# Values projected as rows of keys in one product with the keys, their step found by folds and two TensorE transposes

## The reference

```python
q = (x @ Wq + bq).reshape(1, B * N, H, hd)
kv = (cond @ Wkv + bkv).reshape(1, -1, 2, H, hd)
k, v = (kv[:, :, 0], kv[:, :, 1])
q = _fq_sym(q, axis=-1)      # rounded to 127 steps of the row's own maximum
k = _fq_sym(k, axis=-1)
v = _fq_sym(v, axis=2)       # one step for each channel, from the maximum over all 5776 keys
attn = jax.nn.softmax(jnp.einsum('bhqd,bhkd->bhqk', q, k), axis=-1)
attn = _fq_unsigned(attn, axis=-1)
out = jnp.einsum('bhqk,bhkd->bhqd', attn, v)
```

## Time and profile before

| | us |
|---|---|
| median of 3 runs | 1885.77 |
| the runs | 1884.38 to 1887.85 |
| the profiled execution, its own time | 1881.91 |
| its span | 1880.1 |
| VectorE busy | 1694.6 (90%) |
| TensorE busy | 1644.0 (87%) |
| GpSimd busy | 1450.3 (77%) |
| ScalarE busy | 1373.7 (73%) |
| 16 DMA engines, share of the span | 79.4% |

### The profile page before, as it was taken

The page is one execution under the profiler, slowest core; times in us unless marked ns, Lnnn a source line. Parts: engine busy times, 40 slices in busy tenths (PEclk is TensorE's granted clock), DMA queues, the critical chain, the costliest instruction groups (busy, mean ns, idle before and its releaser), DMA issues.

```text
span 1880.1 us, 40526 instructions
## 1 busy us (share of the span) xinstructions
PE 1644.0 (87%) x16216; PEld 1131.0 (60%) x16216; DVE 1694.6 (90%) x2665; ACT 1373.7 (73%) x1326; POOL 1450.3 (77%) x1190
## 2 busy tenths in 40 slices
PE   7997889888898888889888888888988888789998
PEld 6884666665566666655666666444455455468776
DVE  6869999999999999999999999999999999986665
ACT  2447889888888988887888888877778888732222
POOL 1442899988999988989989889899898799652232
PEclk9999999997699999977999999756589999889999
DMA  5668889997999799969897999798988998841231
GB/s 175 214 209 200 173 171 206 190 191 149 177 189 194 158 199 181 189 139 193 171 207 159 177 189 200 123 172 161 175 167 160 190 194 160 162 117 44 66 58 46
DMA packets 851527, 309.88 MB, mean 165 GB/s; under 512 B 784966, under 2 KB 813964, under 8 KB 851212
## 3 DMA queue, kind: packets, MB, share of 16 engines
q1 hardware_dynamic: 851340, 307.29, 79.4%
HBM read 74.26 MB, written 39.59 MB: 61 GB/s over the span
## 4 chain that ended last, share of the span: by engine, by line
DVE 44%; PE 22%; POOL 11%; DMA 8%; issue 7%; ACT 6%; SPq 1%; POOLq 0%; DVEq 0%; ACTq 0%
DVE S L1159 39%; POOL PT L1388 8%; DMA PP<-Pr 6%; PE PS L776 5%; ACT Pr L973 4%; PE PS L657 4%; PE PK L813 3%; PE PK L598 2%; PE PS L625 2%; PE PK L600 1%; PE PO L600 1%; PE PO L598 1%; POOL VV L1333 1%; PE PO L676 1%; DVE kam L1058 1%
## 5 line engine op out<-in xcount | busy, mean ns | idle before, releaser
L1159 DVE TENSOR_SCALAR_CACHE_REDUCE S<-PS,SQN 128x1536 f32<-128x1536 f32 (+1 forms) x768 | 1285.0, 1713 | 45.1 <-PE PS L657 37.5
L973 ACT ACTIVATE Pr<-S,MS 128x5888 uint8<-128x5888 f32 x200 | 1041.3, 5207 | 207.2 <-DVE MJ L1185 143.1
L1388 POOL CAST PT<-PP 128x1536 uint16<-128x1536 uint8 (+1 forms) x800 | 1100.7, 1420 | 112.0 <-DMA PP<-Pr 109.3
L657 PE MATMUL PS<-KT,QT 96*128 96x512 bf16 (+1 forms) x2496 | 711.7, 410 | 141.5 <-DVE S L1159 127.3
L676 PEld LDWEIGHTS PO<-VI,PT 128*128 128x128 f16 x9200 | 354.1, 99 | 226.0 <-issue 79.7
L657 PEld LDWEIGHTS PS<-KT,QT 96*128 96x128 bf16 (+1 forms) x2496 | 206.3, 104 | 354.4 <-issue 164.0
L676 PE MATMUL PO<-VI,PT 128*128 128x32 bf16 x9200 | 365.5, 180 | 11.4 <-ACT AO L923 8.0
L598 PE MATMUL PK<-WG,CT 128*128 128x128 f32 (+1 forms) x1288 | 217.9, 300 | 46.1 <-ACT VV L839 38.8
L600 PE MATMUL PK<-CT,WG 128*128 128x128 f32 (+1 forms) x1288 | 213.2, 294 | 0.0
L598 PEld LDWEIGHTS PK<-WG,CT 128*128 128x128 f32 (+1 forms) x1288 | 171.8, 197 | 52.4 <-issue 51.2
L600 PEld LDWEIGHTS PK<-CT,WG 128*128 128x128 f32 x1288 | 168.5, 194 | 1.7 <-issue 0.6
(11 more groups left out here) (149 smaller groups left out, 1501.6 us busy)
## 6 DMA issues: line engine op xcount, KB each, us to landing
CT<-ctxt SPq DMA_DIRECT2D x180, 256.0 KB, 3.2
k_rows<-KS SPq DMA_DIRECT2D x44, 512.0 KB, 4.1
q_rows<-QS SPq DMA_DIRECT2D x13, 512.0 KB, 4.2
W13F<-w13T SPq DMA_DIRECT2D x12, 352.0 KB, 3.7
PP<-Pr SPq DMA_TRANSPOSE x200, 5.9
XT<-x SPq DMA_DIRECT2D x12, 256.0 KB, 3.3
XR<-x SPq DMA_DIRECT2D x12, 256.0 KB, 3.4
base_rows<-XO SPq DMA_DIRECT2D x12, 256.0 KB, 3.4
```

The lines of the kernel that those rows point to most:

```text
L657: last = pe.matmul(PS[n % 2][p0:p0 + r, f:f + w], QT[h % 3][0:PARTS * HD, q0:q0 + r], KT[h % 3][0:PARTS * HD, c * CHUNK + f:c * CHUNK + f ...
L973: act.activation(Pr[i % 2].rearrange("p t q b -> p t b q"), S[i % 2].rearrange("p (t b q) -> p t b q", b=2, q=P), ACT.Exp, bias=MS[:, i % ...
L1159: v.tensor_scalar(S[i % 2][:, c * CHUNK:c * CHUNK + CW[c]], PS[n % 2][:, 0:CW[c]], neg_step, None, ALU.mult, ALU.min, accum_out=MN[:, i % ...
L1388: gp.tensor_copy(PT[i % 2][:, 2 * t0:2 * t1, :].rearrange("p (t b) q -> p t b q", b=2), PP[i % 2][:, t0:t1, :].bitcast(U8).rearrange("p t ...
```

## The change

- **One product for keys and values.** A unit is now four float32 products with the context as the stationary operand and 256 columns, 128 of key weights and 128 of value weights, and one bias product of 256 columns before the last of them. Values come out as rows of keys, as the product with the attention weights wants them. The last unit is padded to 128 rows. The bias tiles are twice as wide; VectorE makes the parts of group 0 first and those of the other groups (768 columns) after the second `layernorm`.
- **The step of a channel.** Channels now lie along the row. `batch` takes the maximum over the four units of a batch for each of 128 channels (512 elements in, 128 out, the inner step 512 bytes), into one of five slots of `VM`. After batches 3, 6, 9 and 11 VectorE folds four slots into one (`V_FOLD`, again 512 in, 128 out, behind the last chunk of the step). TensorE transposes the 128x128 of maxima (`max_turn`), `v_step` reduces it out of PSUM, ScalarE spreads the reciprocal over a row (`scale_spread`), TensorE transposes it back (`scale_turn`) and ScalarE copies the row of scales to `VS` (`scale_out`).
- **Rounding.** `v_quant` is now a multiplication of two tensors (values by the broadcast `VS`) and the addition and subtraction that rounds, written straight to `VI`. It begins 1.2 steps later. Group 0 is rounded by it too, on GpSimd, 12 batches at the end of the front.
- **Removed:** the 36 DMA transposes of `turn_v`, the three of group 0 with ScalarE's `value_ints`, four small loads of the values' bias, four memsets of `VB` on GpSimd.

```diff
-                for c in slices:
-                    for d in range(2 * (c % 2), 2 * (c % 2) + 2):
-                        if c < 2:
-                            pe.matmul(bank[0:n, 0:GC], CT[k % RING][:, d, 0:n], WG[:, d, 0, :], start=(d == 0), stop=False)
-                        else:
-                            last = pe.matmul(bank[:, GC:GC + n], WG[:, d, 1, :], CT[k % RING][:, d, 0:n],
-                                             start=(d == 0), stop=(d == NK - 1))
...
+                for d in slices:
+                    last = pe.matmul(bank, CT[k % RING][:, d, :], WG[:, d].rearrange("p a c -> p (a c)"),
+                                     start=(d == 0), stop=(d == NK - 1))
+                    if d == NK - 2:
+                        if u == 0 and g < 2:
+                            pe.wait_ge(M["s_b3"], g + 1)
+                        pe.matmul(bank[0:n], ones[:, 0:n], BK3[:, 2 * GC * g:2 * GC * (g + 1)], start=False, stop=False)
...
+            def max_turn(g):
+
+                pe.wait_ge(M["s_vm"], len(V_FOLD) * (g + 1))
+                pe.wait_ge(M["s_kve"], (g + 1) * NU)
+                pe.transpose(v_bank(g)[:, 0:GC], VM[:, 0, :], ident[:, :]).then_inc(M["s_vmt"], 1)
+
+            def scale_turn(g):
+
+                pe.wait_ge(M["s_vbc"], g + 1)
+                pe.transpose(v_bank(g)[:, GC:2 * GC], VM[:, 1, :], ident[:, :]).then_inc(M["s_vst"], 1)
...
-                        for r in range(VRING if g else 0):
-                            pe.wait_ge(s_vb[r], 16 * (NBT * g // VRING))
-                        pe.wait_ge(M["s_vi"], 16 * len(VT_LO))
+                        pe.wait_ge(M["s_vg"], NBT * (g + 1))
...
+                    if i in v_step_of and c == 2:
+                        max_turn(v_step_of[i])
+                    if i - 2 in v_step_of and c == 1:
+                        scale_turn(v_step_of[i - 2])
...
+            def scale_spread(g):
+
+                act.wait_ge(M["s_vr"], g + 1)
+                act.wait_ge(M["s_vmt"], g + 1)
+                act.activation(VM[:, 1, :], ones[:, :], ACT.Copy, scale=VS3[:, g % 2, 2:3]).then_inc(M["s_vbc"], 1)
+
+            def scale_out(g):
+
+                act.wait_ge(M["s_vst"], g + 1)
+                if g:
+                    act.wait_ge(M["s_vg"], NBT * g)
+                act.activation(VS, v_bank(g)[:, GC:2 * GC], ACT.Copy).then_inc(M["s_vs"], 1)
...
-                vals = VV[b][:, 0:w] if g else VF[:, us[0] * P:us[0] * P + w]
-                chain.mark(v.tensor_reduce(VMX[:, g % 2, b:b + 1], vals, X, ALU.max, apply_absolute_value=True))
+                vals = VV[b] if g else VF[:, us[0]:us[-1] + 1, :]
+                slot = b if b < NB else (b - NB) % (NB - 1) + 1
+                if b == 0 and g:
+                    v.wait_ge(M["s_vst"], g)
+                chain.mark(v.tensor_reduce(VM[:, slot, :], vals.rearrange("p n c -> p c n"), X, ALU.max,
+                                           apply_absolute_value=True))
...
+                if b in V_FOLD:
+                    lo = V_FOLD.index(b) % 2
+                    v.tensor_reduce(VM[:, (1 - lo) * NB, :], VM[:, lo:lo + NB, :].rearrange("p n c -> p c n"), X,
+                                    ALU.max).then_inc(M["s_vm"], 1)
+                    v.wait_ge(M["s_vm"], len(V_FOLD) * g + V_FOLD.index(b) + 1)
...
             layernorm(0)
             layernorm(1)
+            bias_parts(1, NG)
...
-                        if b == NBT - 1:
-                            v_step(0)
+                    if t == Q_HEAD + 1:
+                        v_step(0)
...
-                    gp.wait_ge(M["s_vr"], g + 1)
-                link(gp.tensor_scalar(q, q, VS3[:, g % 2, 2:3], MAGIC, ALU.mult, ALU.add))
-                if k >= NBT + VRING:
-                    gp.wait_ge(s_vb[k % VRING], 16 * ((k - NBT) // VRING))
-                gp.tensor_scalar(VB[k % VRING][:, 0:w], q, 1.0, -MAGIC, ALU.mult, ALU.add).then_inc(M["s_vg"], 1)
+                    gp.wait_ge(M["s_vs"], g + 1)
+                    if g >= 2:
+                        gp.wait_ge(M["s_pv"], PHASE * (g - 1))
+                link(gp.tensor_tensor(q, q, VS.unsqueeze(1).to_broadcast([P, n, GC]), ALU.mult))
+                gp.tensor_scalar(VI[g % 2][:, us[0]:us[-1] + 1, :], q, MAGIC, -MAGIC, ALU.add, ALU.add).then_inc(M["s_vg"], 1)
...
-            for a in range(VRING):
-                link(gp.memset(VB[a], 0.0))
+            for b in range(NBT):
+                v_quant(0, b)
+            gp.wait_ge(M["s_vg"], NBT)
...
-                             (end + 4.95 + b * 2 / 3, v_quant, (g, b))]
+                             (end + 6.15 + b * 2 / 3, v_quant, (g, b))]
```

More of the change, by code:

```diff
@@ L189, in build @@
         KS = tmp("KS", [NB, GH, P], BF16)
-        VV += [tmp(f"VV{b}", [NB * P], F32) for b in range(2, 5)]
-        VB = ring("VB", VRING, [NB * P], BF16)
+        VV += [tmp(f"VV{b}", [NB, GC], F32) for b in range(2, 5)]
+        VM = tmp("VM", [NB + 1, GC], F32)
+        VS = tmp("VS", [GC], F32)
         WG = tmp("WG", [NK, 2, GC], F32)
@@ L222, in build @@
         with ExitStack() as early:
[L223 removed]
+            VV += [tmp(f"VV{b}", [len(BATCH[b]), GC], F32, early) for b in range(5, NBT)]
         with ExitStack() as early:
@@ L283, in build @@
         s_w2 = [sem(f"s_w2{n}") for n in range(len(W2_SPLIT))]
-        s_vb = [sem(f"s_vb{r}") for r in range(VRING)]
         block = ctx.enter_context(nc.Block())
@@ L316, in build @@
                 dve_batches.setdefault(STEP_OF_UNIT[g, us[-1]] + 2, []).append((g, b))
-        v_step_of = {STEP_OF_UNIT[g, NU - 1] + 4: g for g in range(1, NG)}
-        v_turns = {}
-        for g in range(1, NG):
-            for b in range(NBT):
-                v_turns.setdefault(STEP_OF_UNIT[g, NU - 1] + 5 + b * 2 // 3, []).append((g, b))
+        group_end = {g: STEP_OF_UNIT[g, NU - 1] for g in range(1, NG)}
+        v_step_of = {end + 3: g for g, end in group_end.items()}
+        v_bank = lambda g: PK if g else PO
         @block.sync
@@ L909, in _ @@
                 if t == Q_HEAD + 1:
+                    scale_spread(0)
                     k_high(0, NBT - 1)
-            for n in range(len(VT_LO)):
-                value_ints(n)
+                if t == Q_HEAD + 2:
+                    scale_out(0)
             def values_out(i):
@@ L1178, in _ @@
                                          ZB[:, pr * PAIRT:(pr + 1) * PAIRT]).then_inc(M["s_rz"], 1)
+                    if c == NC_ - 1 and i in v_step_of:
+                        v_step(v_step_of[i])
                     if i == NA - 1 and c == NC_ - 2:
```

132 lines of the change are left out of this document (53 added, 79 removed).

## The result

The changed kernel takes 1957.12 us (median of 4 runs, 1953.88 to 1960.99), against 1885.69 us for the kernel before on the same chip: a ratio of 1.0378, 95% interval 1.0357 to 1.0400. Forecast were 1897 us, and a range that ended at 1912. The sign was right, the size was not: 71 us instead of 11. The profiled execution has a span of 1959.2 us, against 1880.1.

What follows compares the result with a forecast made beforehand. VectorE, with 44% of the chain, was taken to bound the kernel. Front +4.3 us and attention +7.3 us made +11.6 us: 1893.5 us in the profiled execution's terms, 1897 us as a median, range 1878 to 1912.

Steps and rivals of the forecast that it cites:

- additions on VectorE are paid one for one: Attention steps: whatever VectorE gets in addition is paid in full, unless it was going to wait in that step.
- The front, +4.3 us: Everything before the attention: units -2.3, start +2.7, fold and `v_step` +0.8, last two queries +3.1 us.
- taken 2.7: Start of the front: bias parts for 768 columns on VectorE delay ScalarE's root and the first query, +2.7 us.
- taken -0.05: Front, TensorE: change per unit of products, -0.05 us, times 46 gives -2.3 us.
- taken at 0.8: End of the front, VectorE: one fold +0.7 us and a wider reduction in `v_step` +0.1 us.
- taken 3.1: End of the front: the last two queries on VectorE run beside GpSimd's rounding of group 0, +3.1 us.
- The second stays: GpSimd's rounding of values: the second operation keeps its old time, 0.60 us.
- L1345, 1.01 us: GpSimd's multiplication by a broadcast, priced by L1301 at 1.01 us against 0.67 for the operation it replaces.
- Boundaries, 0: Three group boundaries: GpSimd's extra work offset by the 1.2-step delay and SP's freed queue; 0, ends -12 and +9 us.
- Strided reads, the rival of 0.11: VectorE's maxima and folds at 512 bytes' distance run at half speed, 0.68 us more each: +33 us, 1930 us; chance 0.11.
- Relief: Boundaries: SP's queue without transposes of values lets GpSimd carry its extra work; 1879 us, chance 0.20.
- nothing much: Folds hide by more than half, GpSimd's front rounding costs queries nothing, bias parts are absorbed: 1887 us; chance 0.19.

Runs made afterwards that it cites:

- a_nofold: a_both with each of the folds replaced by a one-element operation: 1895.12 us, ratio 1.0070 to the kernel before.
- a_rowscale: a_both with GpSimd's old first operation on values (multiply by one number a row, add MAGIC), leaving out channel scales: 1874.69 us, ratio 0.9938.
- b_src: Kernel before, with unused tiles so that only the source of the probabilities' transposes begins at a multiple of 256 bytes: 1868.52 us, ratio 0.9918.
- a_both: Changed kernel with multiply-add instead of two additions (no rounding to whole steps), and maxima and folds reading elements in a row: 1897.57 us, ratio 1.0080.
- b_dst: Kernel before, with an unused tile so that only the destination of the probabilities' transposes begins at a multiple of 256 bytes: 1888.53 us, ratio 1.0029.
- a_ileave: Changed kernel, rounding in three exact operations, units of a channel side by side: maxima read in a row, ScalarE and GpSimd stride 16 bytes; 1934.97 us, ratio 1.0282.
- b_pad192: Kernel before, with an unused tile of 192 bytes ahead of the large buffers, so packed probabilities begin at a multiple of 256 bytes: 1872.24 us, ratio 0.9916.
- a_multadd: Changed kernel with GpSimd's second rounding operation as multiply by 1, add 0 instead of two additions, leaving out rounding to whole steps: 1912.34 us, ratio 1.0119.

## Why the prediction was wrong, point by point

- **What bounds the kernel, and that additions on VectorE are paid one for one**: right. 15 to 18 of the 18 us of slower reductions were paid, and the folds, at 0.53 us more than what stands in their place in a_nofold, in full.
- **The front, +4.3 us**: near in sum, +5.5, of which 1.7 was not in it. The third tile's root came 1.4 us later and VectorE's first query 2.9 (taken 2.7). A unit fell from 1.90 us to 1.84 (taken -0.05), so that the query at 120 us was only 1.1 us late. Behind the last units this had grown by 0.4, where fold and `v_step` had been taken at 0.8; the last two queries took 5.51 and 5.21 us in the changed kernel where they took 4.2 and 4.1, and the copy 0.4 more, +2.9 together (taken 3.1). Not foreseen was TensorE's clock, +1.7.
- **"The second stays"**: this is the step that failed. The diff turned a multiplication and an addition into two additions, on the same shape and types, and the prediction gave them the price of the old form, 0.60 us. It is 1.92, and this one term is 45 to 47 us of the 71. No row of before had the new form, so it should have had a bound from both sides, as the maxima had.
- **L1345, 1.01 us**: mis-sized; 1.27. L1301 is 1.05 in the shape with 512 columns, and a nearer row was overlooked: L1345 of the kernel before, a subtraction of two whole rows of 512 numbers without a broadcast, took 1.21 us.
- **Boundaries, 0**: wrong. With 1.27 for 0.70 the boundaries lose 19 to 22 us, GpSimd's extra work in full. The 1.2 steps of gap and SP's freed queue were to absorb it; a_rowscale, which has both, stands at 94.4, 115.3 and 91.4 us, and b_src, which has neither, at 94.4, 115.3 and 92.8. Together they come to a microsecond or two there; no run takes either by itself. A place where one engine is already late has no slack to hide in, and the prediction had said so itself (7.6 against 6.8).
- **What it had not seen**: the tiles of the transposes moved to a multiple of 256 bytes, which gives back 14 to 16 us by the kernel before. This and the boundaries cancelled, and so a_both met the sum: by luck. Smaller gains went unseen too: outside the boundaries, steps 111 and 119 take 7.2 and 8.2 us in a_both, but 8.4 to 8.5 and 9.7 to 11.1 in the kernel before, b_src and b_dst. Why was not looked into.
- **Strided reads, the rival of 0.11**: the mechanism was right. The price is 0.39 us a reduction instead of 0.68, and 15 to 18 us instead of 33; a step with a fold took 9.4 us, where 8.8 were to show it. The 16-byte lines of the Trainium skill ("SBUF — State Buffer", section "Door 1: The DMA port swizzle"), weighed in the prediction, agree with VectorE's 1.07 against 0.68 us; the page doesn't say how much a crossing costs. For GpSimd the Trainium skill states such a rule too ("GPSIMD Engine Reference", section "7. Performance pitfalls for Q7 kernels": reads at a step of more than 8 bytes take half as long again); a_ileave shows 1.11 against 0.62 us, 80% more.
- **Relief and "nothing much"**: neither came.

From before to after by the medians, then: the place of the source -14 to -16; folds, bias parts, start and units, from b_pad192 to a_rowscale, +2.5; the multiplication +20 to +23; the distance of reads +15; two additions in the place of a multiplication and an addition +45 to +47. Together +67 to +74, measured 71. That the sum comes out is no proof of the terms, since each run of this chain (b_pad192, a_rowscale, a_both, a_multadd) differs from the next in one of them. By the table's ratios the same chain reads -16, +4, +27, +7 and +49: a term is known to some 4 us, that of the reads to 8, and there the steps (17 us) decide.

## What to carry to other kernels

An instruction that keeps its operands but changes its pair of operations is a new instruction: look for its form in the trace, and if it isn't there, give it two bounds. When two runs differ by less than their noise, compare the steps that hold the edit. Extra work on an engine that is already late at a stage is paid in full there, and relief elsewhere is not its counterweight until a wait of that stage names it. A change of tile sizes also moves every tile behind it, and where a DMA transpose reads from SBUF, put its source at a multiple of 256 bytes.

## What the runs showed of the hardware that was not expected

- GpSimd at 128x512, float32 to bf16: multiply-add 0.62 us, add-add 1.93 us. Two multiply-adds (1.24) are faster than one add-add.
- A transpose from SBUF to SBUF: 4.4 us at the least with its source at a multiple of 256 bytes, 5.3 with 64 or 128 bytes more; the destination's place had no effect.
- The last two queries of the front, VectorE's work: 4.2 and 4.1 us alone, 6.5 and 6.9 beside GpSimd's multiplications and roundings.
- Distance of accesses, 512 float32: VectorE's maximum 0.68 to 1.07 us at 512 bytes; GpSimd 0.62 to 1.11 at 16 bytes; ScalarE's write of 128 elements 275 to 392 ns at 16 bytes.
- TensorE's clock after one and the same pause of 3.9 us: full in one kernel, a mean grant of 0.65 in another. Why it falls in the one and not in the other was not settled.
